# A fused linear-attention and mixture-of-experts kernel: head states kept as full 128x128 blocks instead of 64-column halves, and the routing ranks issued behind the queries

## The reference

```
xn = layernorm(x)
q, k, v = split(xn @ W_qkv)            # 16 heads of 8 features
k = layernorm_per_head(k)
for chunk in 16 chunks of 64 tokens:   # per sequence and head
    inter = S @ q_c
    intra = causal(q_c k_c^T) @ v_c
    y_c = inter + intra
    S = S + v_c^T k_c                  # the 8x8 state of a head
attn = y @ W_o
e = argmax(xn @ centroids.T)           # one of 8 experts per token
ffn = gated expert MLP (128 -> 512 -> 128) of expert e on xn
out = x + attn + ffn
```

## Time and profile before

| | |
|---|---|
| median of 3 runs | 363.04 us (362.52 to 364.0) |
| the profiled execution | 363.22 us |
| its span, from the first to the last recorded instruction | 361.4 us |
| TensorE, matmuls | busy 94% of the span |
| VectorE | busy 78% |
| ScalarE | busy 67% |
| GpSimd | busy 69% |
| mean granted TensorE clock | 0.992 |

### The profile page before, as it was taken

One profiled execution on the slowest core, in us unless ns is written; L12 is line 12 of the kernel. 1 busy time (PEld: TensorE's weight loads), 2 busy tenths in 40 slices (PEclk: granted clock), 3 DMA queues, 4 the chain that ended last, 5 costly groups with the idle time before them and its releaser, 6 DMA issues. The chain is left out here.

```text
span 361.4 us, 17478 instructions
## 1 busy us (share of the span) xinstructions
PE 341.2 (94%) x6868; PEld 293.5 (81%) x6868; DVE 283.6 (78%) x799; ACT 241.7 (67%) x657; POOL 250.2 (69%) x245
## 2 busy tenths in 40 slices
PE   7799999989899999999999989999999999999990
PEld 7466776777587787777877878999999999999990
DVE  8887898898785988977878786788887778877760
ACT  4788677777667657666665735766677667766660
POOL 3388567889886865455455503888887888888884
PEclk9999999999999999999999999999999999999996
DMA  7403213021433233255233225555555555555420
GB/s 203 103 22 92 63 38 86 26 77 54 128 98 92 91 93 91 82 149 152 93 99 100 78 58 137 69 72 72 68 64 77 72 76 67 70 75 61 37 23 0
DMA packets 46705, 28.99 MB, mean 80 GB/s; under 512 B 5096, under 2 KB 44320, under 8 KB 46624
## 3 DMA queue, kind: packets, MB, share of 16 engines
q1 hardware_dynamic: 34352, 19.34, 19.6%
q0 software_dynamic: 12272, 8.54, 17.1%
HBM read 14.53 MB, written 13.78 MB: 78 GB/s over the span
## 5 line engine op out<-in xcount | busy, mean ns | idle before, releaser
L495 POOL DMA_INDIRECT out_dram<-qx,rows x71 | 112.7, 1588 | 36.0 <-issue 21.9
L695 ACT ACTIVATE qx<-sc,b1T 128x128 f32<-128x128 f32 x280 | 79.8, 368 | 40.4 <-PE sc L1424 40.4
L421 POOL DMA_INDIRECT slots_d<-rows,pos_i x64 | 62.8, 981 | 41.3 <-PE bank L1331 10.7
L857 DVE TENSOR_TENSOR pr<-sc,causal 128x1536 f32<-128x1536 f32 (+2 forms) x33 | 63.5, 1926 | 16.3 <-PE sc L1277 16.2
L1432 PE MATMUL bank<-tokens,qx 128*128 128x128 f32 x568 | 75.2, 276 | 0.7 <-ACT qx L695 0.7
L1424 PE MATMUL sc<-wide,tokens 128*128 128x128 f32 x560 | 74.1, 275 | 0.4 <-issue 0.4
L1432 PEld LDWEIGHTS bank<-tokens,qx 128*128 128x128 f32 x568 | 69.0, 192 | 1.1 <-ACT qx L695 1.1
L1424 PEld LDWEIGHTS sc<-wide,tokens 128*128 128x128 f32 x560 | 68.2, 192 | 0.6 <-issue 0.6
L1016 DVE COPY tokens<-xT 128x1024 f32 x71 | 53.3, 752 | 0.2 <-issue 0.2
L1277 PEld LDWEIGHTS sc<-qx,kT 32*64 32x64 f32 x2048 | 32.9, 130 | 16.8 <-issue 16.4
L1031 DVE SCALAR_TENSOR_TENSOR qx<-bank,rows,qx 128x128 f32<-128x128 f32 x71 | 24.8, 350 | 27.2 <-PE bank L1432 26.5
(11 more groups left out here) (167 smaller groups left out, 531.4 us busy)
## 6 DMA issues: line engine op xcount, KB each, us to landing
rows<-slots_d SPq DMA_DIRECT2D x71, 66.0 KB, 2.0
out_dram<-tokens SPq DMA_DIRECT2D x16, 256.0 KB, 2.7
tokens<-in_L_attn_x_dram SPq DMA_DIRECT2D x7, 512.0 KB, 4.2
w1raw<-in_L_ffn_w_dram SPq DMA_DIRECT2D x8, 256.0 KB, 3.3
w2raw<-in_L_ffn_w_dram SPq DMA_DIRECT2D x8, 256.0 KB, 2.9
out_dram<-qx,rows POOLq DMA_INDIRECT x71, 3.4
slots_d<-rows,pos_i POOLq DMA_INDIRECT x64
slots_d<-empty SPq DMA_DIRECT2D x9, 66.0 KB
```

The costliest lines, as they stand in the source:

```text
L421: pool.indirect_dma_start(slots_d, bass.IndirectOffsetOnAxis(ap=pos_i[:, t:t + 1], axis=0), rows[:, t, :], None)\
L495: pool.indirect_dma_start(out_rows, bass.IndirectOffsetOnAxis(ap=xs[:, a, D + 2:D + 3].bitcast(U32), axis=0), ye[:, a, :], None, bounds_ch ...
L695: last = nc.scalar.activation(ht[:, k % 2, c * P:(c + 1) * P], inner(k)[:, c * P:(c + 1) * P], ACT.Relu, bias=b1T[:, bass.ds(e * FC + c, 1)])
L857: nc.vector.tensor_tensor(pr[:, h % 2, a:G, w].rearrange("p g (j t) -> p g j t", t=CH), sc[:, a * BANK:G * BANK].rearrange("p (g w) -> p g ...
```

## The change

`state`, `smid` and `dstate` get 128 columns instead of 64, and `headmask` (128x128) takes the place of `smask`. `state_step` makes one product over all 128 features for each sequence and chunk instead of two over 64. `inter_first` and `inter_second` use one matmul over all 128 partitions instead of two over 64. Since the state step now fills `FA`, the ranks move to `Y[0]`; on TensorE `rank_tokens` goes from ahead of `state_step` to behind `q_project`, with a wait for the result of the quad before to be read out of `Y[0]`. `output` of quad 8 moves to the even half (`out_early`). On VectorE `ranks`, `places` and `tiles_of_experts` move behind `result`. `affT` shares memory with `sq`, and two broadcast loads trade places in `tokens`, one of them two quads earlier.

```diff
-        GW = 64
-        state = sb("state", [P, B, GW])
-        smid = sb("smid", [P, HALF, GW])
-        dstate = sb("dstate", [P, NC, HALF, GW])
-        smask = sb("smask", [P, GW])
+        state = sb("state", [P, B, D])
+        smid = sb("smid", [P, HALF, D])
+        dstate = sb("dstate", [P, NC, HALF, D])
...
-        affT = sb("affT", [P, HALF * P])
+        affT = sq
...
-        RANK = HALF * GW
+        RANKS = Y[0]
...
-            return n % 2 == 1 and n < 9
+            return n % 2 == 1 and n < 11
...
-                if n == 6:
+                if n == 4:
                     stored(n - 1)
                     sp.dma_start(lbb, ln_b.partition_broadcast(P)).then_inc(s("lb_in"), 16)
...
-            nc.vector.tensor_reduce(out=smask[:, :], in_=headmask[:, :].rearrange("p (g k) -> p k g", k=GW), axis=AX,
-                                    op=ALU.add)
...
-                nc.vector.tensor_tensor(dstate[:, 0, :, :], Y[n % 2][:, 0:HALF * GW].rearrange("p (i k) -> p i k", k=GW),
-                                        bcast(smask[:, :], 1, HALF), ALU.mult).then_inc(s("dsta_sb"), 1)
+                nc.vector.tensor_tensor(dstate[:, 0, :, :], Y[n % 2][:, :].rearrange("p (i k) -> p i k", k=D),
+                                        bcast(headmask[:, :], 1, HALF), ALU.mult).then_inc(s("dsta_sb"), 1)
...
-                    if n in (3, 5, 7, 9):
-                        ranks(n // 2 - 1)
                     if n >= LATE:
                         state_steps(n)
...
                     if n and out_early(n):
                         result(n - 1)
+                    if n in (3, 5, 7, 9):
+                        ranks(n // 2 - 1)
+                        places(n // 2 - 1)
+                    if n == LATE:
+                        tiles_of_experts()
...
-                if n in (3, 5, 7, 9):
-                    rank_tokens(n // 2 - 1)
                 for i in range(HALF):
-                    for a in range(P // GW):
-
-                        for c, bank in ((0, Y[n % 2]), (1, FA))[:2 if n < NQ - 2 else 1]:
-                            r, k = slice(CH * c, CH * (c + 1)), slice(i * D + GW * a, i * D + GW * (a + 1))
-                            last = mm(bank[GW * a:GW * (a + 1), i * GW:(i + 1) * GW], kn[r, n % 2, k], vp[r, k], start=True,
-                                      stop=True)
+
+                    for c, bank in ((0, Y[n % 2]), (1, FA))[:2 if n < NQ - 2 else 1]:
+                        r, k = slice(CH * c, CH * (c + 1)), slice(i * D, (i + 1) * D)
+                        last = mm(bank[:, k], kn[r, n % 2, k], vp[r, k], start=True, stop=True)
...
-                        for a in range(P // GW):
-                            r = slice(GW * a, GW * (a + 1))
-                            last = mm(Y[half][r, i * P:i * P + CH], state[r, half * HALF + i, :],
-                                      qT[r, half, i * P:i * P + CH], start=(i == 0), stop=False)
+                        last = mm(Y[half][:, i * P:i * P + CH], state[:, half * HALF + i, :], qT[:, half, i * P:i * P + CH],
+                                  start=(i == 0), stop=False)
...
+                pe.wait_ge(s("res_ready"), 2 * b + 3)
+                to = RANKS[:, 0:BATCH * E]
...
                     if more:
                         q_project(n + 1)
+                    if n in (3, 5, 7, 9):
+                        rank_tokens(n // 2 - 1)
```

More of the change, by code:

```diff
@@ L1286, in bank_y_free @@
                     pe.wait_ge(s("aff_sb"), n // 2)
+                if n % 2 == 0 and 4 <= n <= 10:
+                    pe.wait_ge(s("rank_sb"), n // 2 - 1)
             def inter_first(n):
@@ L1306, in inter_second @@
                 for i in range(HALF):
-                    for a in range(P // GW):
-                        r = slice(GW * a, GW * (a + 1))
-                        last = mm(Y[half][r, i * P + CH:(i + 1) * P], smid[r, i, :], qT[r, half, i * P + CH:(i + 1) * P],
-                                  start=False, stop=False)
+                    last = mm(Y[half][:, i * P + CH:(i + 1) * P], smid[:, i, :], qT[:, half, i * P + CH:(i + 1) * P],
+                              start=False, stop=False)
                 last.then_inc(s("inter_ps"), 1)
```

24 lines of the change are left out of this document (10 added, 14 removed).

## The result

The changed kernel takes **380.65 us** (median of 4 runs, 378.93 to 381.41) where the one before takes 363.38 in the same runs: a ratio of 1.0471 (1.0436 to 1.0506), or +17.1 us. The profiled execution, 378.93, was the fastest of the four. The forecast was 378 with a range of 367 to 384. The time came out close, but several terms of the sum were wrong in size and made up for each other; most of what follows is about that.

A forecast was written before the change was run, and what follows sets the result against it. The prediction took TensorE to bound the loop, with VectorE close behind. Its terms, 12.7 - 0.6 - 0.3 + 1.2 + 2.3 = +15.3 us on the profiled 363.22, gave 378 us, range 367 to 384.

The forecast's parts named there:

- The prices of TensorE's groups: TensorE per quad: state step +0.47 us, `inter_first` +0.28, `inter_second` +0.08, together +0.83.
- The late quads: Quads 10 to 13: the odd mask, `vp` and weight copies come later than TensorE's added 0.83 us; about 1.1 longer each.
- the other side: Rival, 11%: 480 fewer records and three fewer switches per quad outweigh wider columns; 6% faster, 5% within 0.5%.
- -0.6: Three places where `inter_first` waits for `dstate`: the longer state step is swallowed, only +0.27 us comes through; -0.6 us.
- +1.2: Quads 10 to 13: VectorE's chain comes 1.2 us later, TensorE 0.83; the difference cut to 0.3 each, +1.2 us in all.
- +2.3: Quad 9: moved ranks delay the mask and `vp`, TensorE waits for `vp` and its copy; +2.3 us beyond its own 0.83.
- the term for VectorE and GpSimd: Wider `dstate` on VectorE and wider additions on GpSimd: costed at -0.6 us, nothing, and +1.2 in the late quads.
- nothing: GpSimd's two additions, +1.07 us in quads 2 to 8, lie behind TensorE's longer stretch; costed at nothing.
- a microsecond added to TensorE in a quad is a microsecond on the end: The loop: TensorE bounds it, so its added time reaches the end, unless it falls in one of few waits.
- +12.7 us: Wide products on TensorE: +0.83 us in 14 quads, 0.55 each in quads 0 and 1; +12.7 us.
- `rank_tokens` itself costs TensorE the same in either place: Moving `rank_tokens` behind `q_project` adds no TensorE time of its own.
- The -0.3 for the mask that isn't built: Start of the kernel: the mask no longer built saves 281 ns, -0.3 us.

The follow-up runs named there:

- e7: Changed kernel with each full-height matmul of both inter-chunk sets cut into two of 64 weight columns, all 128 rows kept; 379.24 us, 1.0411.
- e11: Kernel before with every `q_project` matmul issued twice in each quad, nothing else changed; 372.75 us, 1.0247.
- e1: Changed kernel with the state step alone put back to 64x64 products; 379.45 us, 1.0418.
- e12: Changed kernel with each state-step matmul cut to its first 64 features, same matmul count, states of heads 8 to 15 left out; 377.66 us, 1.0395.
- e2: Changed kernel with both inter-chunk sets, `inter_first` and `inter_second`, put back to 64x64 products; 379.21 us, 1.0435.
- e3: Changed kernel with the state step and both inter-chunk sets put back to 64x64; wide VectorE and GpSimd work and new order stay; 375.18 us, 1.0329.
- e6: Kernel before with only `state`, `smid`, `dstate` and the mask 128 wide, upper columns zero; TensorE's instructions and order unchanged; 372.52 us, 1.0215.
- e5: Kernel before with the new order alone: ranks in `Y[0]`, `rank_tokens` behind `q_project`, VectorE's rank work behind `result`; 369.85 us, 1.0143.
- e4: Changed kernel with quad 9's rank and expert work moved on VectorE to behind the odd half's `v_scale`; 376.02 us, 1.0344.
- e9: Kernel before with 8 of its 22 idle warm-up transposes on TensorE left out; 364.4 us, 1.0027.
- e8: e4 with `b1_fold` of all late quads also moved into the odd half on VectorE; 378.77 us, 1.0424 against the kernel before.
- e10: Kernel before with `tiles_of_experts` of quad 9 and `b1_fold` of quads 8 to 13 moved to the odd half on VectorE; 363.77 us, 1.0017.

## Why the prediction came out right in time and wrong in its terms

*What held.* The prices of TensorE's groups: state step 1.09 (predicted 1.09), `inter_first` +0.28, `inter_second` +0.08 with the switch, 0.20 us for each change of tile shape, loads of 128 columns as the pace of the sets (e7). The 688 ns of VectorE and 1281 ns of GpSimd. Quad 9, +3.2 us where 2.3 and its own 0.83 were predicted, by the waits for `vp` and the copy that were named, and one for `qT` that was not. The late quads at 0.3 to 1.1 where about 1.1 was said (the 0.3 is quad 12, which before had a pause of 0.6 in it). The experts unchanged.

*The pauses, which the sum did not have.* TensorE stops in mid-group, with no semaphore, for up to 2.3 us between matmuls and 2.6 between weight loads. I added up the gaps of over 0.25 us between weight loads of one group in the loop, without those that a semaphore ended or that stand between the doubled matmuls of e11: 3.3 us before, nothing in the changed kernel, and 2.7, 3.2, 4.3, 0, 5.7, 4.2, 1.7, 0.4, 3.6, 2.7, 1.4 and 0 in e1 to e12. In kernels with 6868 weight loads the long ones come near numbers 1347, 2350 and 3480 (not each kernel pauses at each), in the three with 6628 (e1, e2, e7) near 1971, and with 6388 there is none over 0.5 us. So the change got some 3 us back where its stream has no pauses: quad 6, which did not grow, is where the long pause of before stood. The rival "the other side" also counted fewer records as a gain, but by cheaper sets and fewer switches; pauses were in none of the rivals. And e1, e2 and e3 gave part of their gain away to pauses.

*The costs with the pauses taken out.* If a pause counts in full at the end, which is an estimate (in e1 one of 1.94 us made quad 5 2.0 longer than in e12; before, the pause of 1.4 us made quad 6 some 1.0 longer than quads 4 and 8, 13.46 against 12.22 and 12.63), each difference to before is corrected by its pauses less 3.3. The pauses are those of one profiled execution and the difference is that of all runs, whose intervals reach 1.3 to 2 us either way, so the column is good to 2 us or so:

```
                               measured   corrected   predicted
all (after)                      +17.1      +20.4       +15.3
VectorE and GpSimd alone (e6)     +7.8       +6.9        +0.3 (-0.6, -0.3, +1.2)
the order alone (e5)              +5.2       +2.8        +2.3
both, no wide product (e3)       +12.0      +11.0        +2.6
wide products (after less e3)     +5.1       +9.4       +12.7
q_project twice (e11)             +9.0      +10.9       of 12.8 on TensorE
```

The stretches at the low clock are not taken out; e5's and e6's profiles have two each that the kernel before has not, which is why the two are rather smaller than the column says.

*What failed first: the term for VectorE and GpSimd.* It was costed at **-0.6**, **nothing** and **+1.2**, and is 6 to 7. The prediction let only quads 10 to 13 pay; in e6 3.0 us come from quads 1 to 5, 7 and 8. But the first `dstate` stands ahead of `inter_first` in the early quads too, and widened, it makes TensorE wait there: 4.9 us of weight-load waits in 6 places in e6 where 2.5 in 3 places were before. The argument that a longer state step swallows such waits holds (the changed kernel has 2.6 us of them in 4 places, e1 and e12 with the short step 5.7 and 5.5 in 8), but it was used to take 0.6 off, when VectorE's own lengthening had to be added first.

*What failed second: "a microsecond added to TensorE in a quad is a microsecond on the end".* The **+12.7 us** was taken whole. Of 12.8 us put on TensorE alone 9.0 arrive, 10.9 corrected (e11); of the 12.7 of the wide products 9.4 corrected (e3); of the 7.5 of the state step's half 2.7, or 3.5 by quads 1 to 14 of the profiles (e12, where neither kernel has a pause). TensorE's groups that start "without a hole" in quad 10 spoke for one quad, not for the loop.

These two belong together. VectorE's 16.9 us more busy time in e6 cost 6 to 7, TensorE's 12.7 some 9: neither engine alone is the bound. Each `inter_first` starts when the later of two chains arrives, TensorE's own row of matmuls or VectorE's `dstate`, and the chain by the mask, `vp` and the weight copy meets TensorE again at `kT_project`. Which is later changes from quad to quad. That is shown for the `dstate` wait, which grows when the state step is cut and shrinks when it is wide; for the second meeting the rows show waits, but no run took that chain apart.

*The order* was costed about rightly: +2.3, against 2.5 by e4 and at most 2.8 by e5. But not all of it is in quad 9: "`rank_tokens` itself costs TensorE the same in either place" did not hold, it costs 0.18 us more in each of four quads.

So 15.3 had 3.3 too much for the products, some 8 too little for the rest as e3 has it, and 3.3 too much for pauses of before that went away and that no term covered. The measured 17.1 is 15.3 with these three set right; the forecast was near by errors that cancelled, and that is luck. It would have failed for a change that widened VectorE's work only.

*The -0.3 for the mask that isn't built* did not show: the first state step starts at 16.1 us in both.

*What stays open.* What sets the pauses and their lengths. At the long one of the kernel before a 16 KB transfer of the instruction queue starts at 96.72 and the pause at 97.56. All the 18 pauses of over 0.5 us in these profiles' loops (again without e11's doubled matmul) end 2.2 to 3.2 us after such a transfer has started, where the transfers come 3.3 to 9.2 us apart. That ties the pauses to the transfers, but most transfers bring none, and the changed kernel has them as well; that TensorE runs out of instructions there is argued, not shown. Nor is it settled why e4's runs gain 4.6 us over the change when its quad 9 gains 2.5 (the clock is the likely rest), and how much of the cost of the wide work is GpSimd's.

## What to carry to other kernels

Where a second engine's chain has no slack, cost each edit on both chains; a probe that loads one engine only (e6, e11) tells what its microsecond is worth, and before two kernels are compared to the microsecond, the pauses in their streams and the stretches at the low clock have to be counted. Merging two half-height matmuls into one of full height saved nothing on TensorE here, because the weights got twice as wide and the columns of the load set the pace (e7). Work moved later in one engine's queue delays everything behind it, also on engines that only queue behind one small result of it, as ScalarE's `qT` behind `kstd`.

## What the runs showed of the hardware

Two things had not been expected. The pauses: 1.16 us ahead of the matmul in the kernel before, 2.31 in e6 at the same load number, 2.04 in e9 one load earlier, 1.94 in e1, and none over 0.5 us in the kernel with 480 records fewer; leaving 8 transposes out moved the work that is hit, not the place in the stream. And the clock: in the profile of e1 one stretch early in the loop has a granted clock of 0.66, where the changed kernel's has 1.00, though TensorE was busy ahead of it and in it:

```profile
17.00:27.00 10.00, 8.36 (x149) 6.12 (x149) 7.79 (x14) 6.57 (x13) 8.38 (x10) 0.66 0.17 50
```

Quad 0 took 14.46 us in that execution and 12.07 in the changed kernel's. The profiles of e5, e6, e9, e10, e11 and e12 have such a stretch as well (0.83 in this window, 0.66 in e12). The clock also fell later on: to 0.50, the 1.2 GHz level, within 1.3 us of the end of long pauses in e3 (quad 9), e5, e6 and e9 (quad 6), and at or just behind waits of TensorE of 1 to 2 us in quad 9 of e1, e2 and e7 and in the last quad of e8. In e9, behind the pause that ends at 102.19, TensorE was busy without a gap and yet had half the clock:

```profile
102.30:105.30 3.00, 3.00 (x66) 2.83 (x67) 0.67 (x2) 1.39 (x3) 2.29 (x3) 0.50 0.02 5
```

Other pauses as long, of 1.69 us between matmuls in e10 and 1.94 in e1, had no such stretch behind them. One costs 1.3 to 1.4 us here: quad 0 takes 12.53 us in e10 and 11.17 in the kernel before, quad 9 17.56 in e1 and 16.25 in e12. So a pause or a wait can cost its own length and such a stretch on top; with the early ones that is a part of the scatter of 1 to 5 us between runs of one kernel, and why e1's difference is read from its interval and not from its profile.
